# One operand of VectorE's small operations moved from SBUF to PSUM in a fused macaron block

## The reference

```
FFN:  shared = silu(x @ Ws_up) @ Ws_down                    # hidden width 64
      aff = x @ centroids.T                                 # 64 experts
      idx = top_k(aff + expert_biases, 8)
      w = sigmoid(aff at idx); w = w / (sum(w) + 1e-8)
      routed = sum over e of cw[:, e] * (silu(x @ W_up[e]) @ W_down[e])   # cw: w at idx, else 0
      y = shared + routed
Attention: softmax(q k^T) * (1/sqrt(128)) @ v, one head
LN:   (x - mean) / sqrt(var + 1e-5)
```

## Time and profile before

| | |
|---|---|
| time, median of 3 runs | 581.1 us (579.74 to 582.62) |
| time of the profiled execution | 577.28 us |
| its span, first to last instruction | 575.4 us |
| first FFN, attention, second FFN | about 0 to 237, 237 to 373, 373 to 575 us |
| TensorE busy | 547.6 us (95%) |
| VectorE busy | 434.4 us (75%) |
| ScalarE busy | 408.3 us (71%) |
| GpSimd busy | 278.2 us (48%) |
| granted TensorE clock, mean | 0.993 |

### The profile page before, as it was taken

How to read it: one execution, slowest core, us unless ns; L and a number is a source line. 1 busy time by engine, 2 the same in 40 slices (tenths; PEclk the granted TensorE clock), 3 DMA queues, 4 the chain that set the end, 5 groups by cost and what they waited for, 6 DMA issues and landing times.

```text
span 575.4 us, 8712 instructions
## 1 busy us (share of the span) xinstructions
PE 547.6 (95%) x2737; PEld 442.6 (77%) x2737; DVE 434.4 (75%) x911; ACT 408.3 (71%) x808; POOL 278.2 (48%) x247
## 2 busy tenths in 40 slices
PE   7689999899989999899999999899999999999997
PEld 5466777677867778679999999778777777877885
DVE  6487679968996676577877978698768968875664
ACT  7667777687768777566666657576876787687774
POOL 3878765766676576200000000065674766566563
PEclk9799999999999999999999999999999999999999
DMA  8535564354545553000000000045554565566652
GB/s 274 159 119 172 165 195 157 126 173 166 169 135 179 179 166 127 0 1 2 1 1 2 0 2 1 1 139 176 173 185 153 169 189 158 168 172 193 186 186 101
DMA packets 44190, 72.22 MB, mean 126 GB/s; under 512 B 8848, under 2 KB 9552, under 8 KB 44144
## 3 DMA queue, kind: packets, MB, share of 16 engines
q1 hardware_dynamic: 43568, 71.17, 38.9%
q10 hardware_dynamic: 512, 0.36, 0.2%
q0 software_dynamic: 64, 0.13, 0.1%
HBM read 69.53 MB, written 2.10 MB: 124 GB/s over the span
## 4 chain that ended last, share of the span: by engine, by line
PE 76%; DVE 11%; POOL 5%; ACT 3%; issue 3%; DMA 0%; POOLq 0%; DVEq 0%; SPq 0%; ACTq 0%
PE lrow L965 11%; PE lrow L966 11%; PE lrow L967 11%; PE bank L1007 9%; PE bank L1009 8%; PE bank L1008 8%; PE bank L1013 5%; PE bank L1205 3%; PE bank L1207 3%; PE bank L1206 3%; POOL gpart_lo L252 2%; DVE rs L650 2%; DVE gated L625 1%; DVE rs L648 1%; PE bank L967 1%
## 5 line engine op out<-in xcount | busy, mean ns | idle before, releaser
L252 POOL TENSOR_TENSOR gpart_lo<-gated,gpart_hi 128x512 fp32r<-128x512 f32 x174 | 223.9, 1293 | 190.3 <-ACT gpart_hi L417 186.4
L406 ACT ACTIVATE lrow<-lrow 128x512 f32<-128x512 f32 (+1 forms) x252 | 147.3, 585 | 61.4 <-PE lrow L967 60.9
L625 DVE TENSOR_TENSOR gated<-lrow,wide 128x512 f32<-128x512 f32 x166 | 114.0, 687 | 47.2 <-ACT lrow L406 43.5
L417 ACT CAST gpart_hi<-gated 128x512 fp32r<-128x512 f32 x174 | 106.5, 613 | 7.5 <-DVE gated L625 6.8
L1007 PE MATMUL bank<-gpart_lo,wdn_hi 128*128 128x512 f32 x256 | 102.4, 400 | 6.5 <-POOL gpart_lo L252 6.3
L1009 PE MATMUL bank<-gpart_hi,wdn_hi 128*128 128x512 f32 x256 | 101.8, 398 | 0.0
L1008 PE MATMUL bank<-gpart_hi,wdn_lo 128*128 128x512 f32 x256 | 101.4, 396 | 0.0
L625 DVE TENSOR_TENSOR lrow<-lrow,wide 128x512 f32<-128x512 f32 x78 | 54.2, 694 | 29.8 <-ACT lrow L406 29.6
L417 ACT CAST gpart_hi<-lrow 128x512 fp32r<-128x512 f32 (+1 forms) x90 | 53.2, 591 | 31.0 <-DVE lrow L625 30.8
L1007 PEld LDWEIGHTS bank<-gpart_lo,wdn_hi 128*128 128x128 f32 x256 | 48.3, 189 | 21.3 <-issue 5.3
L252 DVE TENSOR_TENSOR gpart_lo<-lrow,gpart_hi 128x512 fp32r<-128x512 f32 (+1 forms) x90 | 61.4, 682 | 2.8 <-ACT gpart_hi L417 2.1
(11 more groups left out here) (209 smaller groups left out, 996.4 us busy)
## 6 DMA issues: line engine op xcount, KB each, us to landing
wide<-gates_dram SPq DMA_DIRECT2D x488, 128.0 KB, 3.0
raw<-in_w_up SPq DMA_DIRECT2D x8, 256.0 KB, 5.3
raw<-in_w_down SPq DMA_DIRECT2D x8, 256.0 KB, 5.5
gates_dram<-gates SPq DMA_DIRECT2D x8, 128.0 KB, 2.3
x<-in_x SPq DMA_DIRECT2D x3, 256.0 KB, 4.1
out_dram<-x SPq DMA_DIRECT2D x3, 256.0 KB, 3.0
x<-in_x SPq DMA_DIRECT2D x1, 128.0 KB, 2.3
x<-in_x ACTq DMA_DIRECT2D x1, 128.0 KB, 2.5
```

The costliest lines, as they stand in the source:

```text
L252: return eng.tensor_tensor(gpart[1][0:m, U % NGP, :], gated_at(U)[0:m, :], gpart[0][0:m, U % NGP, :].bitcast(F32), ALU.subtract)
L406: nc.scalar.activation(dst[0:m, :], hid[U % NH][0:m, :], ACT.Silu).then_inc(s_silu, 1)
L417: nc.scalar.copy(gpart[0][0:m, U % NGP, :], gated_at(U)[0:m, :]).then_inc(s_ghi, 1)
L625: nc.vector.tensor_tensor(gated_at(U), a, b, ALU.mult).then_inc(s_gated, 1)
```

## The change

Seven edits.

1. `normed` (k = 0 and 1, not the one inside the attention): var + eps is made once more by VectorE, into PSUM; the Newton step's operand ve, its intermediate t and its result r lie in `mp[:, 256:280]`. The tiles are made by scalar_tensor_tensor with r broadcast from PSUM as a tensor operand, in place of tensor_scalar with r as a second pointer scalar from SBUF.
2. The `normed` of pass 4, inside the attention, keeps its form as `attention_normed`.
3. TensorE waits before `pro_xT` until all four tiles are there (for n = 1, 2, 3, 5, 6, 7), since r lies in the bank that it is about to write.
4. ScalarE writes silu of the affinity to `mp[:, 0:256]`, and so waits until the biased affinity has been read from there.
5. L699 becomes one scalar_tensor_tensor, (rest == LOWEST) * silu, with the silu from PSUM and the product in `sil`; for pass 4 it is (rest == LOWEST) * rec, all in SBUF.
6. `weights` on GpSimd is one multiplication, rec * sil; for pass 4 (`chosen`, on VectorE) likewise one instead of two.
7. `pro_sum` leaves the sum in PSUM before it adds 1e-8 (in bank 0 for pass 0, in SBUF for pass 4).

```diff
             def weights(n):
-                pool.wait_ge(p_sil, n + 1)
                 pool.wait_ge(p_top, n + 1)
-                link(nc.gpsimd.tensor_tensor(rec[:, :, :], rec[:, :, :], sil[:, :, :], ALU.mult))
-                nc.gpsimd.tensor_tensor(rec[:, :, :], rec[:, :, :], rest[:, :, :], ALU.mult).then_inc(p_w, 1)
+                nc.gpsimd.tensor_tensor(rec[:, :, :], rec[:, :, :], sil[:, :, :], ALU.mult).then_inc(p_w, 1)
...
             def pro_sil(n):
-                act.wait_ge(p_affs, n)
-                nc.scalar.activation(sil[:, :, :], aff[n // NCH][:, :, :], ACT.Silu).then_inc(p_sil, 1)
+                if n == NCH:
+                    act.wait_ge(p_affs, n)
+                else:
+                    act.wait_ge(p_bias, n)
+                dst = flat(sil) if n == NCH else mp[:, 0:TPC * E]
+                nc.scalar.activation(dst, flat(aff[n // NCH]), ACT.Silu).then_inc(p_sil, 1)
...
-            def normed(k, n, c, dst, ready, done, tiles=range(TPC)):
+            def newton(k, ve, t, r):
+                y = rs[:, k, 1, :]
+                link(nc.vector.tensor_tensor(t, y, ve, ALU.mult))
+                link(nc.vector.scalar_tensor_tensor(out=t, in0=t, scalar=-0.5, in1=y, op0=ALU.mult, op1=ALU.mult))
+                link(nc.vector.scalar_tensor_tensor(out=r, in0=t, scalar=1.5, in1=y, op0=ALU.add, op1=ALU.mult))
+            def normed(k, n, c, dst, ready, done, tiles):
+                ve, t, r = (mp[:, TPC * E + (3 * k + i) * TPC:TPC * E + (3 * k + i + 1) * TPC] for i in range(3))
                 if 0 in tiles:
                     dve.wait_ge(ready, n + 1)
-                    ve, y, t, r = (rs[:, k, i, :] for i in range(4))
-                    link(nc.vector.tensor_tensor(t, y, ve, ALU.mult))
-                    link(nc.vector.scalar_tensor_tensor(out=t, in0=t, scalar=-0.5, in1=y, op0=ALU.mult, op1=ALU.mult))
-                    link(nc.vector.scalar_tensor_tensor(out=r, in0=t, scalar=1.5, in1=y, op0=ALU.add, op1=ALU.mult))
+                    dve.wait_ge(s_gates, n if k == 0 else n + 2)
+                    link(nc.vector.tensor_scalar(ve, mv[:, k, :, 1], EPS, None, ALU.add))
+                    newton(k, ve, t, r)
                 for i in tiles:
-                    nc.vector.tensor_scalar(dst[:, i, :], x[:, c * TPC + i, :], mv[:, k, i, 0:1],
-                                            rs[:, k, 3, i:i + 1], ALU.subtract, ALU.mult).then_inc(done, 1)
+                    nc.vector.scalar_tensor_tensor(out=dst[:, i, :], in0=x[:, c * TPC + i, :], scalar=mv[:, k, i, 0:1],
+                                                   in1=r[:, i:i + 1].to_broadcast([P, D]), op0=ALU.subtract,
+                                                   op1=ALU.mult).then_inc(done, 1)
...
                     link(ins)
-                    nc.vector.tensor_tensor(rest[:, :, :], rest[:, :, :], b[:, :, :], ALU.not_equal).then_inc(p_top, 1)
+                    if n == NCH:
+                        out = other = rec[:, :, :]
+                    else:
+                        dve.wait_ge(p_sil, n + 1)
+                        out, other = sil[:, :, :], mp[:, 0:TPC * E].rearrange("p (t e) -> p t e", e=E)
+                    nc.vector.scalar_tensor_tensor(out=out, in0=rest[:, :, :], scalar=LOWEST, in1=other,
+                                                   op0=ALU.is_equal, op1=ALU.mult).then_inc(p_top, 1)
...
             def chosen(n):
-                link(nc.vector.tensor_tensor(rec[:, :, :], rec[:, :, :], sil[:, :, :], ALU.mult))
-                nc.vector.tensor_tensor(rec[:, :, :], rec[:, :, :], rest[:, :, :], ALU.mult).then_inc(p_w, 1)
+                nc.vector.tensor_tensor(rec[:, :, :], rec[:, :, :], sil[:, :, :], ALU.mult).then_inc(p_w, 1)
...
             def pro_sum(n):
                 dve.wait_ge(p_w, n + 1)
-                link(nc.vector.tensor_reduce(wsum[:, 0, :], rec[:, :, :], AX, ALU.add))
-                link(nc.vector.tensor_scalar(wsum[:, 0, :], wsum[:, 0, :], 1e-8, None, ALU.add))
+                total = (mp if n else bank[0])[:, TPC * E:TPC * E + TPC] if n != NCH else wsum[:, 0, :]
+                link(nc.vector.tensor_reduce(total, rec[:, :, :], AX, ALU.add))
+                link(nc.vector.tensor_scalar(wsum[:, 0, :], total, 1e-8, None, ALU.add))
                 nc.vector.reciprocal(wsum[:, 1, :], wsum[:, 0, :]).then_inc(p_inv, 1)
...
             def pro_xT(n):
                 if n:
                     pe.wait_ge(s_gates, n)
+                if n % NCH:
+                    pe.wait_ge(p_xn, TPC * (n + 1))
                 turn_tiles(xn[n // NCH], mp, p_xn, n, p_xT)
```

More of the change, by code:

```diff
@@ L641, in stats, with attention_normed @@
                 ins.then_inc(done, 1)
-            def normed(k, n, c, dst, ready, done, tiles=range(TPC)):
+            def newton(k, ve, t, r):
[5 more added lines that the diff above has]
+                ve, t, r = (mp[:, TPC * E + (3 * k + i) * TPC:TPC * E + (3 * k + i + 1) * TPC] for i in range(3))
                 if 0 in tiles:
                     dve.wait_ge(ready, n + 1)
-                    ve, y, t, r = (rs[:, k, i, :] for i in range(4))
-                    link(nc.vector.tensor_tensor(t, y, ve, ALU.mult))
-                    link(nc.vector.scalar_tensor_tensor(out=t, in0=t, scalar=-0.5, in1=y, op0=ALU.mult, op1=ALU.mult))
-                    link(nc.vector.scalar_tensor_tensor(out=r, in0=t, scalar=1.5, in1=y, op0=ALU.add, op1=ALU.mult))
+                    dve.wait_ge(s_gates, n if k == 0 else n + 2)
+                    link(nc.vector.tensor_scalar(ve, mv[:, k, :, 1], EPS, None, ALU.add))
+                    newton(k, ve, t, r)
                 for i in tiles:
-                    nc.vector.tensor_scalar(dst[:, i, :], x[:, c * TPC + i, :], mv[:, k, i, 0:1],
-                                            rs[:, k, 3, i:i + 1], ALU.subtract, ALU.mult).then_inc(done, 1)
+                    nc.vector.scalar_tensor_tensor(out=dst[:, i, :], in0=x[:, c * TPC + i, :], scalar=mv[:, k, i, 0:1],
+                                                   in1=r[:, i:i + 1].to_broadcast([P, D]), op0=ALU.subtract,
+                                                   op1=ALU.mult).then_inc(done, 1)
+            def attention_normed():
+                dve.wait_ge(p_rs, NCH + 1)
+                newton(0, *(rs[:, 0, i, :] for i in (0, 2, 3)))
+                for i in range(TPC):
+                    nc.vector.tensor_scalar(xn[1][:, i, :], x[:, i, :], mv[:, 0, i, 0:1],
+                                            rs[:, 0, 3, i:i + 1], ALU.subtract, ALU.mult).then_inc(p_xn, 1)
             def last_normed():
@@ L924, in _ @@
                         if t == T_XT:
-                            normed(0, NCH, 0, xn[1], p_rs, p_xn)
+                            attention_normed()
                         for j in range(KB):
```

## The result

The changed kernel took 565.33 us in the median (564.21 to 565.79, 4 runs), the kernel before 580.98 on the same chip: ratio 0.974, 95% interval 0.9706 to 0.9774. The prediction had 569.1, a ratio of 0.979. A second measurement gave 564.57 (7 runs) beside 579.61 (11 runs), ratio 0.9736 (0.9707 to 0.9764). So the gain is 15 us, with 2 us of uncertainty, where 12.0 was worked out. More than the sum had been given a chance of 0.05. The profiled execution took 565.64, its span is 563.9.

A forecast was written before the change was run, and what follows sets the result against it. TensorE, with 76% of the chain that ended last, was taken to bound the kernel. Terms 3.3 + 2.5 + 4.4 + 0.8 + 1.0 = 12.0 us off 581.1 gave 569.1; own range 566.5 to 571.5, wide range 565.5 to 575.0.

The forecast's parts named there:

- More than the sum: Case of a larger gain, as VectorE's freed time may end small waits left out; chance 0.05.
- Who ends the stalls, and why they are late: In the FFNs late norm tiles end TensorE's stalls; VectorE operations with two SBUF tensors wait out GpSimd's instruction.
- First norms: First norm: a stall of 0.83 us goes in passes 1, 2, 5, 6 (3.3 us), and 2.5 in pass 0.
- the cover: First norm: 0.97 us in hand before TensorE begins its transposes, so the wait for four tiles costs nothing.
- Second norm and choice: Second norm, passes 1 and 2: stalls of 2.43 us go, 0.2 given back; 2.2 each, 4.4 us.
- The allowance of 0.2 for GpSimd: Second norm, passes 1 and 2: 0.2 us given back for TensorE's need of GpSimd's L252.
- GpSimd's multiplication: Pass 0: one multiplication less takes 0.8 us off TensorE's wait for GpSimd's queue; elsewhere it is cover.
- The sum at the start: Ahead of pass 0: L758's hold goes and the first gates come 1.0 us sooner; nothing in the passes.
- The price for PSUM reads in the Trainium skill: Rule against the change: an estimated 65 ns an instruction; second norms 0.5 us late twice, sum 11.0.
- GpSimd taking over: Rival, passes 1 and 2: TensorE waits 1.3 us for GpSimd, twice; 571.3 us; chance 0.20, shared with some stall staying.
- Slow broadcast: Rival, norm tiles: r broadcast from PSUM makes a tile cost 1.28 us instead of 0.26; 595 us; chance 0.03.
- No hold lifted: Rival, norms: the hold isn't one of operands; 1 to 2 us saved, 1 to 2 paid; 581 us; chance 0.06.

The follow-up runs named there:

- the probe: No part of the block: twelve kinds of VectorE operation timed with GpSimd idle and running 128x512 operations without a pause; no time of the block.
- e4: The changed kernel with the same instructions, every operand that went to PSUM back in SBUF: 581.74 us, ratio 1.0049 to the kernel before.
- e1: The kernel before with edits 1 to 3 alone (the norms and TensorE's wait for four tiles): 569.52 us, ratio 0.9836.
- e2: The kernel before with edits 4 to 6 alone (silu to PSUM, merged choice, one GpSimd multiplication less): 575.10 us, ratio 0.9945.
- e3: The kernel before with edit 7 alone (sum of the weights left in PSUM before 1e-8 is added): 578.31 us, ratio 0.9993.
- e9: The changed kernel once more, unaltered, beside the kernel before: ratio 0.9736.
- e10: The changed kernel with pass 0's reciprocal of the sum in PSUM too: 564.18 us beside the changed kernel's 564.57.
- e8: The changed kernel with r in SBUF, tiles by tensor_scalar as before and no wait for four tiles: 568.70 us, ratio 0.9812.
- PRE = 3: The changed kernel with three weight pieces instead of six ahead of GpSimd's first low parts: 561.11 us, ratio 0.9679.

## Why the prediction was right, point by point

*Who ends the stalls, and why they are late.* Right, and shown: the probe gives the hold alone, and e4, with the same instructions and only the places changed, loses all of the gain. The Trainium skill (SBUF — State Buffer, "Terms", the entry "shared port pair") says that VectorE and GpSimd share a pair of SBUF ports as an exclusive lock for a whole instruction, and that the loser blocks; the probe agrees, 1.19 us instead of 0.16 beside an operation of 1.26.

*First norms.* Right to 0.01 us in the chain of operations (0.80) and the cover (0.96). The terms of passes 5 and 6 were 0.83 and measured 1.0; pass 4, put at nothing, gave 0.5, and pass 3 with the attention 0.7. Of the 1.0 the norms alone give 0.86 (e1) and the choice 0.2 (e2). These are small waits that the prediction left out, since they show in no bracket: the row of the matmul ahead covers them. The 0.7 are two of them in pass 3, both before L1007, both ended by GpSimd's low part. The first, in the kernel before:

```profile
211.21 1.29 POOL L252 TENSOR_TENSOR gpart_lo<-gated,gpart_hi 128x512 fp32r<-128x512 f32 x1 [2.19 <-ACT gpart_hi L417]
...
212.55 0.50 PE L1007 MATMUL bank<-gpart_lo,wdn_hi 128*128 128x512 f32 x1
```

The low part ends at 212.50. L1007 starts 0.40 behind the matmul ahead of it instead of 0.23, and its row is 0.50 instead of 0.40. This wait costs 0.3 us, the second, at 215.74, 0.4, and neither is left in the changed kernel.

*Second norm and choice.* Right: 3.0 for a pass against 0.83 + 2.2. The allowance of 0.2 for GpSimd was used by VectorE's low part (0.31) instead.

*GpSimd's multiplication.* Right in kind, 0.2 too small. The prediction calls the wait of 0.86 + 0.16 short of L346's 0.74 and its link; it is longer than these, and all of it went, in e2 and in the changed kernel. With pass 0's first norm 3.3 were forecast and 3.5 measured.

*The sum at the start.* Wrong in size: 1.0 forecast, 0.1 measured between the two traces, 0.4 in e3. The timeline of the changed kernel at the first gates:

```profile
13.19 1.29 POOL L339 TENSOR_TENSOR wdn_lo<-raw,wdn_hi 128x512 fp32r<-128x512 f32 x1 [3.13 <-ACT wdn_hi L470]
13.31 0.16 DVE L782 TENSOR_SCALAR wsum<-bank 128x4 f32<-128x4 f32 x1
...
13.72 0.82 DVE L774 TENSOR_TENSOR rest<-rec,wsum 128x48 fp32r<-128x48 f32 x1
```

L782 is short (0.16), and 0.4 us later L774, two SBUF operands, takes what is left of the same GpSimd instruction: 0.82 instead of 0.21. The term took the whole hold off the chain, but GpSimd's instruction goes on, and the next operation of the held kind meets it. From the biased affinity to the first gates it was 5.32 us before; it is 4.94 in the changed kernel, 4.93 in e9's trace and 4.91 in e3, so the edit gave 0.4 each time. e10 frees L774 too and has 4.33, the 1.0 forecast. The 0.3 by which the changed kernel's trace gains less here than e3's comes with a lower clock of TensorE. Windows of the changed kernel, TensorE (stretch and length, busy, clock, DMA share, GB/s):

```profile
10.00:15.00 5.00, 5.00 (x17) 0.72 1.00 381
...
25.00:30.00 5.00, 4.88 (x12) 0.51 0.62 190
```

From 10 to 15 us it was granted 0.72, so part of the time at the lower of its two levels, 1.2 GHz, and busy throughout; the kernel before has 1.00 there, with waits.

*What the sum doesn't hold.* The passes of the two traces give 12.8, the runs 15.0. The sum was made against one execution of the kernel before, 577.28, and that was a quick one: 2.3 us under the median of its 11 later runs (576.99 to 582.40). The changed kernel's profiled execution, 565.64, is 1.1 over its own median of 564.57. Of these 3.4 us, 1.3 are the loads ahead of the first transposes (they start at 5.33 in the trace of before, at 5.7 to 6.7 in all the others). For the other 2.2 us there are only the mean clocks of the runs: 0.991 in the median of those 11, 0.997 in that of the 7, where the two profiled executions have 0.993 and 0.990. Among the 11, the four at 0.988 took 580.5 to 582.4 us and the three at 0.994 577.0 to 579.6, so 0.006 of clock could be worth such an amount. It isn't shown. The first measurement has the same ratio with the changed kernel's clocks at 0.990 to 0.997, and the listed clock misses slow stretches, as e9 shows. How much of the 2.2 us is clock, and where, stays open. The interval's half width is 1.6 us.

*The price for PSUM reads in the Trainium skill (VectorE: DVE Perf Modes, "The TRN2 errata").* Not borne out. L97 with a PSUM input takes 158 ns, L95 without 162; L109 348, and L111, the same with the broadcast from SBUF, 352 with GpSimd idle. The estimated 65 ns an instruction isn't there.

*The rivals.* GpSimd taking over: no wait on it in passes 1 and 2. Slow broadcast: 343 ns a tile. No hold lifted: e4 is what that would have looked like, 581.7 for the 581 given.

## What to carry to other kernels

Where VectorE and GpSimd work side by side, look for VectorE operations whose longest time is GpSimd's operation, not their own; one tensor operand in PSUM, or the output for tensor_scalar, frees them, even for four elements. Free all of a chain: a hold taken from one operation falls on the next with two SBUF inputs, and two holds before the same wait are worth more together than apart (3.0 us a pass for 1.75 and 0.5). A wait added for the new buffer is free only where TensorE comes later than the tiles: here 0.96 us later in pass 1, while the same wait in the kernel before cost 1.5 us in all. Measure that cover in each pass; e8 lost 1.2 us in the one where it was short. And look for waits of TensorE that stand in no bracket, by matmul rows that are longer than their neighbours.

## What the runs showed of the hardware that I had not expected

- Two SBUF inputs are held even when the output is in PSUM (1186 ns against 170 with GpSimd idle), and not beside a memset, so it is reads of both engines that meet there.
- A GpSimd memset, which reads nothing, holds only tensor_scalar from SBUF to SBUF (451 ns against 170, tiles 505 against 346); two SBUF inputs stay at 164.
- Reading from PSUM in four-element operations is no slower than from SBUF (158 and 162 ns).
- After 4.50 us of idle the changed kernel's TensorE was granted 0.51 in the window from 25 to 30 us; after 0.84 us, with PRE = 3, it kept 1.00. In the nine traces with those 4.50 us the slow matmuls behind them number 7 to 12, so two traces differ by up to 1 us there for no reason of the kernel.
